# One turn of attention outputs for two or three heads instead of one for each, and the first head's shift rows ahead of the second head's masks

## Chip, core and metric

One Trainium2 chip, and of it one core. The metric is the device time of one execution in microseconds (us), given as the median of the runs. Five engines work side by side and wait for each other by semaphores: TensorE (PE), VectorE (DVE), ScalarE (ACT), GpSimd (POOL) and SyncE (SP), which here only issues DMAs.

## What is computed

`x` is 16 batches of 512 rows of 128 features. A feed-forward step with quantized operands, attention with 16 heads of 8 features, and the feed-forward step again:

```python
scores = jnp.einsum('bhqd,bhkd->bhqk', Q, K) / scale        # hd = 8, L = 512
mask = _tpms_mask(L, phase, threshold, temperature)         # one 512x512 mask per head, the same for all batches
scores = scores + TPMS_WEIGHT * jnp.log(mask + 1e-06)[None]
attn = jax.nn.softmax(scores, axis=-1)
out = jnp.einsum('bhqk,bhkd->bhqd', attn, V)
out = out.transpose(0, 2, 1, 3).reshape(B, L, H)
return out @ Wo + bo
...
x = x + 0.5 * _L0_ffn_ref(_layernorm(x, axis=-1), L0_ffn_weight, L0_ffn_bias)
x = x + _L0_attn_ref(_layernorm(x, axis=-1), ...)
x = x + 0.5 * _L0_ffn_ref(_layernorm(x, axis=-1), L0_ffn_weight, L0_ffn_bias)
```

## The kernel before

A prologue computes the logarithms of the 16 masks (ACT, `ln_mask`, L825) and stores each to DRAM (`store_mask`, SP), since its place in the big buffer `BIG` is used for other things later: the places of heads 9 to 12 become the second half of `E`, the exponentials of every odd turn, one batch each. The same prologue projects the first four batches and stores their split queries and keys (`q_parts`, `k_parts`).

Then follow 64 **head turns** `m` = 0 to 63: four quarters of four batches (`j` = 0 to 3), 16 heads each. A turn has eight steps `k`, two for each batch, one for each half ("pair") of the 512 keys:

- DVE copies the log mask into the four banks of `S_PS` (`seed`, L1227): two copies for pair 0 once exponential 6 of the turn before is done, two for pair 1 once exponential 7 is.
- PE adds the scores on top (`scores`, L1656), two matmuls a step. ACT takes the exponential of 1,024 elements a partition into `E` (`exp_step`, L777). Only when exponential `k` has read its banks can the scores of step `k+2` be added.
- At the odd steps PE also multiplies the exponentials of the turn before with the values (`weighted`, L1670): four matmuls, one for each batch, into strips of the bank `O_PS` that start at partitions 0, 32, 64 and 96. Float32 matmuls appear as two records each, so such a set is eight records. A strip has nine rows: eight features and the sum of the exponentials, which comes from a column of ones in the values `VX`.
- Two turns later the output of the head is **turned**: ACT copies `O_PS` to `OTS` (`o_copy`, L786) ahead of exponential 0, PE transposes it in four pieces into `R_PS` (`turn_o`, L1679) at step 1 ahead of the scores, and DVE takes reciprocals of the sums and multiplies (`o_norm`, L1240 and L1242) into `AT`. Only after the copy may PE write the next head's output to `O_PS`.

The order of all work on each engine is written out: at fixed ticks (eight to a turn) each engine's program has its pieces of the neighbouring quarters' layer norms, quantization, projections and output products (`background`, the tables `FIRST`, `LATE`, `SECOND`, `LAST`). Engines work strictly in that order.

The attention starts when PE has the stack of queries and keys of head 0 in `KT` and `QT`. POOL issues these six loads (`load_stack(pool, 0)`), and behind them, when DVE has signalled `bound_copied`, four small loads of head 0's **shift rows** from `OTS` (L659). SP meanwhile stores the masks of heads 9, 10, 11 and 12, and then loads head 1's stack. ACT may write the first exponential of turn 1 when all four of these masks are stored:

```python
if k == 0 and m < 2:
    lnm_stored(act, (6, 9)[m])
```

## Time and profile before

| | |
|---|---|
| median of 3 runs | 875.57 us (873.08 to 876.89) |
| the profiled execution | 872.85 us, of which the span from first to last instruction is 871.0 us |
| PE busy | 741.7 us (85% of the span) |
| ACT busy | 669.0 us (77%) |
| DVE busy | 569.6 us (65%) |
| POOL busy | 192.8 us (22%) |
| first exponential of turn 0 begins | 132.64 us |
| exponentials (L777) | 512, of 1,024 ns |
| mean granted TensorE clock | 0.952 of 2.4 GHz |

Busy times are the union of an engine's records; a matmul record holds its way through the array, so that neighbouring records overlap and a busy PE is not a full one. "[0.31 <-PE S_PS L1656]" behind a row says that the engine stood idle for 0.31 us before it, and that the instruction of that line ended the wait. PEld is PE's weight load, SPq a DMA issue on SP.

### The profile page before, as it was taken

The page shows a single profiled execution, that of the slowest core. Times are in us where ns is not written, and L with a number is a line of the kernel's source. Part 1 is how long each engine was busy: PE and PEld are TensorE (multiplying, and loading weights), DVE is VectorE, ACT ScalarE, POOL GpSimd, SP SyncE. Part 2 cuts the span into 40 slices and gives each one's busy share as a digit, 9 for nine tenths or more (in the row PEclk, how much of TensorE's full clock was granted, in tenths as well). Part 3 has the DMA queues.
Part 4 walks back from the last instruction along what each step waited for, and adds up shares of the span by engine and source line. Part 5 has one row for each costly group of instructions (what it writes and reads, how often), then busy time and mean ns, then how long its engine had stood idle before and what let it go on. Part 6 is the DMA issues. An engine that isn't in the chain of part 4 may idle for free.

```text
span 871.0 us, 13076 instructions
## 1 busy us (share of the span) xinstructions
PE 741.7 (85%) x4355; PEld 260.3 (30%) x4355; DVE 569.6 (65%) x1464; ACT 669.0 (77%) x799; POOL 192.8 (22%) x167
## 2 busy tenths in 40 slices
PE   0575808999998999999999999999999998999844
PEld 0142401333233323333332233223322332331234
DVE  8968885757989746899783565985423458433265
ACT  1567667788887888888888888887888887888711
POOL 0404762003443203164140031441200002000011
PEclk9986856999999999999999999999999999999987
DMA  5539588854666574756857547668676555456101
GB/s 148 124 124 340 199 295 283 284 178 156 201 203 219 184 201 166 194 177 177 249 186 235 175 138 217 195 184 236 199 234 181 172 176 183 145 189 205 38 2 53
DMA packets 56166, 162.11 MB, mean 186 GB/s; under 512 B 14210, under 2 KB 24594, under 8 KB 45674
## 3 DMA queue, kind: packets, MB, share of 16 engines
q1 hardware_dynamic: 51740, 154.36, 57.8%
q0 software_dynamic: 1904, 5.94, 2.0%
q10 hardware_dynamic: 2446, 0.89, 0.5%
q8 instruction: 37, 0.61, 0.3%
q14 instruction: 39, 0.32, 0.1%
HBM read 117.86 MB, written 43.29 MB: 185 GB/s over the span
## 4 chain that ended last, share of the span: by engine, by line
PE 54%; DVE 22%; ACT 11%; issue 9%; DMA 2%; POOL 1%; SPq 0%; DVEq 0%; POOLq 0%; ACTq 0%
PE S_PS L1656 20%; PE O_PS L1670 18%; ACT BIG L777 9%; PE F_PS L1557 5%; DVE S_PS L1227 5%; PE R_PS L1679 3%; PE F_PS L1552 2%; DVE SC L1064 1%; PE P_PS L1557 1%; PE P_PS L1594 1%; DVE ST L954 1%; DVE XC L1109 1%; DVE BIG L1054 1%; PE P_PS L1598 1%; DMA BIG<-OTS 1%
## 5 line engine op out<-in xcount | busy, mean ns | idle before, releaser
L777 ACT ACTIVATE BIG<-S_PS 128x1024 f32<-128x1024 f32 x512 | 508.7, 1024 | 107.0 <-PE S_PS L1656 104.9
L1656 PE MATMUL S_PS<-BIG 98*128 98x512 bf16 x1024 | 311.1, 389 | 40.1 <-DMA BIG<-OTS 15.4
L1227 DVE COPY S_PS<-BIG 128x512 f32<-128x512 f32 x256 | 159.6, 687 | 178.1 <-ACT BIG L777 175.9
L1670 PE MATMUL O_PS<-BIG,VX 128*9 128x512 f32 x2048 | 269.2, 599 | 1.2 <-ACT OTS L786 1.2
L1656 PEld LDWEIGHTS S_PS<-BIG 98*128 98x128 bf16 x1024 | 79.3, 98 | 294.0 <-ACT BIG L777 138.0
L601 POOL TENSOR_TENSOR XDT<-PART 128x512 bf16<-128x512 f32 x24 | 28.9, 1202 | 293.5 <-ACT PART L742 293.5
L1670 PEld LDWEIGHTS O_PS<-BIG,VX 128*9 128x9 f32 x2048 | 30.8, 88 | 103.3 <-issue 99.1
L578 POOL TENSOR_TENSOR X<-X,BFH 128x512 f32<-128x512 f32 x16 | 24.1, 1528 | 149.8 <-DVE BIG L1054 120.3
L818 ACT ACTIVATE BIG<-S_PS,TEMP 128x1024 f32<-128x1024 f32 x32 | 34.1, 1112 | 21.1 <-PE S_PS L1843 20.7
L578 POOL TENSOR_TENSOR BIG<-BIG,BFH 128x512 f32<-128x512 f32 x16 | 19.9, 1270 | 129.1 <-DVE BIG L1054 111.8
L786 ACT ACTIVATE OTS<-O_PS,CON 128x512 f32<-128x512 f32 x64 | 44.1, 689 | 4.4 <-PE R_PS L1679 4.4
L617 POOL TENSOR_TENSOR PART<-PART 128x512 bf16<-128x512 f32 x28 | 36.6, 1306 | 37.6 <-DVE PART L1135 37.6
L1679 PE MATMUL R_PS<-IDENT,OTS 128*128 128x128 f32 x256 | 40.3, 281 | 1.8 <-ACT OTS L786 1.8
L1843 PE MATMUL S_PS<-PART 36*128 36x512 bf16 (+1 forms) x32 | 14.1, 556 | 29.9 <-DMA PART<-trig_parts 27.8
L610 POOL TENSOR_TENSOR PART<-PART 128x512 f32<-128x512 f32 x28 | 35.1, 1254 | 10.6 <-DVE PART L1129 8.3
L711 ACT ACTIVATE XDT<-F_PS 128x512 f32<-128x512 f32 x38 | 22.6, 594 | 18.5 <-PE F_PS L1552 18.5
L1679 PEld LDWEIGHTS R_PS<-IDENT,OTS 128*128 128x128 f32 x256 | 27.7, 141 | 18.4 <-issue 15.2
L1557 PE MATMUL F_PS<-WDT,XDT 128*128 128x128 f32 x208 | 31.9, 300 | 0.0
L1557 PEld LDWEIGHTS F_PS<-WDT,XDT 128*128 128x128 f32 x208 | 27.9, 206 | 12.7 <-ACT XDT L711 7.3
L825 ACT ACTIVATE BIG<-BIG,CON 128x2048 f32<-128x2048 f32 x16 | 30.7, 1987 | 0.0
L1552 PE MATMUL F_PS<-IDENT,BIG 128*128 128x128 f32 x112 | 17.9, 284 | 14.0 <-DVE BIG L1090 10.2
L1240 DVE RECIPROCAL RD<-R_PS 128x16 f32<-128x16 f32 x64 | 16.3, 255 | 17.6 <-PE R_PS L1679 17.1
(197 smaller groups left out, 771.1 us busy)
## 6 DMA issues: line engine op xcount, KB each, us to landing
BIG<-ln_masks SPq DMA_DIRECT2D x62, 1024.0 KB, 6.5
ln_masks<-BIG SPq DMA_DIRECT2D x16, 1024.0 KB, 5.5
BIG<-q_parts SPq DMA_DIRECT2D x63, 192.0 KB
BIG<-k_parts SPq DMA_DIRECT2D x63, 144.0 KB
BIG<-q_parts SPq DMA_DIRECT2D x63, 128.0 KB
q_parts<-PART SPq DMA_DIRECT2D x9, 768.0 KB, 3.8
k_parts<-PART SPq DMA_DIRECT2D x18, 384.0 KB, 4.5
BIG<-k_parts SPq DMA_DIRECT2D x63, 96.0 KB
```

Source lines behind the costliest of these rows:

```text
L578: pool.tensor_tensor(Y, Y, bias[:, None, :].to_broadcast((128, T, H)), ALU.add).then_inc(s[name], 1)
L610: pool.tensor_tensor(F_, F_, hi, ALU.subtract).then_inc(s[f"{q}_r1"], 1)
L617: pool.tensor_tensor(P_[2], F_, P_[1], ALU.subtract).then_inc(s[f"{q}_lo"], 1)
L777: act.activation(E[:, m % 2, j, 2 * pair:2 * pair + 2, :], S_PS[:, pair, :, :], ACT.Exp, scale=LOG_WEIGHT)\
L786: act.activation(OTS[:, :], O_PS[:, :], ACT.Identity, bias=CON[:, 2:3]).then_inc(s["o_copied"], 1)
L818: act.activation(stage(h)[:, 1024 * pair:1024 * pair + 1024].rearrange("p (k l) -> p k l", l=L), S_PS[:, t % 2, :, :], ACT.Sigmoid, scale= ...
L1227: ve.tensor_copy(S_PS[:, pair, i, :], LNM[:, slot, 2 * pair + i, :]).then_inc(s["seeded"], 1)
L1552: mm = pe.transpose(dst[:, 128 * t:128 * t + 128], src[:, t, :], IDENT[:, :])
L1557: mm = pe.matmul(dst[:, 128 * t:128 * t + 128], lhsT[:, 128 * t:128 * t + 128], rhs[:, :], start=True, stop=True)
L1656: mm = pe.matmul(S_PS[:, pair, i, :], KT[0:ALL_ROWS, slot, K_COL[j], 128 * kb:128 * kb + 128], QT[0:ALL_ROWS, slot, j, :], start=False, st ...
L1670: mm = pe.matmul(O_PS[32 * j:32 * j + HD + 1, :], VX[:, slot_of(n), j, kb, h, :], E[:, m % 2, j, kb, :], start=kb == 0, stop=kb == T - 1)
L1679: mm = pe.transpose(R_PS[:, 128 * t:128 * t + 128], OTS[:, 128 * t:128 * t + 128], IDENT[:, :])
```

## The change

**Bunches.** The 16 turns of a quarter fall into six bunches of 3, 3, 3, 3, 2 and 2 turns, and each bunch is turned once, two turns after its last head: 24 turns instead of 64. The heads of a bunch lie below each other in a strip of `O_PS`. For this the stationary operand of the first head of a bunch of three takes 27 columns of the values, its own nine and the 18 ahead of them in memory; it fills rows 0 to 26 of a strip, of which rows 18 to 26 are wanted. The second takes 18 columns and writes over rows 0 to 17, the third takes nine. `VX` gets a pad of 18 columns ahead (`VXP`), and the rows of `Wo` are put in the order in which the heads now stand in `AT`. `o_norm` handles two or three heads at once. A head that is not its bunch's first need not wait for a copy of `O_PS`.

**Start.** The four loads of head 0's shift rows go from POOL's queue to SP's, behind the store of mask 9 and ahead of head 1's stack; masks 10, 11 and 12 are stored behind that. The exponentials of turn 1 wait for the masks batch by batch. In the prologue's list for PE, two mask tiles are computed ahead of `project_k(0, 1)` instead of behind it, and one that stood ahead of `norms_q(0, 1)` stands ahead of `turn_xn(0, 2)`.

```diff
-FIRST_LOADS = 16 * (2 * len(GROUPS) + T)
+FIRST_LOADS = 16 * 2 * len(GROUPS)
...
+BUNCHES = ((0, 2), (3, 5), (6, 8), (9, 11), (12, 13), (14, 15))
+NB = len(BUNCHES)
+MOST = max(b - a + 1 for a, b in BUNCHES)
+VPAD = (MOST - 1) * (HD + 1)
+LAST_HEADS = [b for a, b in BUNCHES]
...
+        def bunch_of(m):
+            return m // NH * NB + len([b for b in LAST_HEADS if b < m % NH])
...
+        def turned_in(m):
+            return bunch_of(m - 2) if m >= 2 and (m - 2) % NH in LAST_HEADS else None
...
-            for h in range(9, 13):
-                store_mask(h)
-
+            store_mask(9)
+
+            sp.wait_ge(s["bound_copied"], 1)
+            for t in range(T):
+                sp.dma_start(QT[QK_ROWS:ALL_ROWS, 0, :, 128 * t:128 * t + 128],
+                             CB4[T * head_of(0) + t:T * head_of(0) + t + 1, :, :, :]).then_inc(s["first_shift"], 16)
             load_stack(sp, 1)
+            store_mask(10)
             load_shift(sp, 1)
-            sp.wait_ge(s["first_stack"], FIRST_LOADS)
+            store_mask(11)
+            store_mask(12)
             store_mask(8)
...
             load_stack(pool, 0)
-
             pool.wait_ge(s["bound_copied"], 1)
-            for t in range(T):
-                pool.dma_start(QT[QK_ROWS:ALL_ROWS, 0, :, 128 * t:128 * t + 128],
-                               CB4[T * head_of(0) + t:T * head_of(0) + t + 1, :, :, :]).then_inc(s["first_stack"], 16)
...
-                if k == 0 and m < 2:
-                    lnm_stored(act, (6, 9)[m])
+                if k == 0 and m == 0:
+                    lnm_stored(act, 6)
+                if pair == 0 and m == 1:
+                    lnm_stored(act, 9 + j)
...
-                    if k == 0 and m >= 2:
-                        o_copy(m - 2)
+                    if k == 0 and turned_in(m) is not None:
+                        o_copy(turned_in(m))
...
-                turned = R_PS[:, :].rearrange("p (t g r) -> p t g r", t=T, g=QB)
-                ve.reciprocal(RD[:, :, :], turned[:, :, :, HD]).then_inc(s["o_rd"], 1)
-                ve.wait_ge(s["o_rd"], m + 1)
-                TT(AT[:, slot_of(n), :, :, HD * h:HD * h + HD].rearrange("p j t d -> p t j d"),
-                   turned[:, :, :, 0:HD], RD[:, :, :, None].to_broadcast((128, T, QB, HD)), ALU.mult)\
+                turned = R_PS[:, :].rearrange("p (t g r) -> p t g r", t=T, g=QB)[:, :, :, 0:size * (HD + 1)]\
+                    .rearrange("p t g (s d) -> p t g s d", s=size)
+                ve.reciprocal(RD[:, :, :, 0:size], turned[:, :, :, :, HD]).then_inc(s["o_rd"], 1)
+                ve.wait_ge(s["o_rd"], u + 1)
+                TT(AT[:, slot_of(n), :, :, HD * first:HD * last + HD].rearrange("p j t (s d) -> p t j s d", s=size),
+                   turned[:, :, :, :, 0:HD], RD[:, :, :, 0:size, None].to_broadcast((128, T, QB, size, HD)), ALU.mult)\
...
-                    if past(m):
-                        pe.wait_ge(s["o_copied"], m)
+                    if past(u) and m % NH == first:
+                        pe.wait_ge(s["o_copied"], u)
                 pe.wait_ge(s["e_ready"], STEPS * m + STEPS - 1 + kb // 2)
                 for j in range(QB):
-                    mm = pe.matmul(O_PS[32 * j:32 * j + HD + 1, :], VX[:, slot_of(n), j, kb, h, :],
+                    at = VPAD + ((j * T + kb) * NH + head_of(m)) * (HD + 1)
+                    mm = pe.matmul(O_PS[32 * j:32 * j + ahead + HD + 1, :],
+                                   VXP[:, slot_of(n), at - ahead:at + HD + 1],
                                    E[:, m % 2, j, kb, :], start=kb == 0, stop=kb == T - 1)
...
-            turn_o(last - 1)
-            turn_o(last)
+            turn_o(bunch_of(last))
```

On SP, at the end of the prologue, before the change (`ln_masks<-BIG` is a mask's store, the six `k_parts` and `q_parts` are head 1's stack, `shift_rows` its shift rows):

```order
L435 DMA ln_masks<-BIG 128x2048 x5
L390 DMA BIG<-k_parts 48x1536
L393 DMA BIG<-q_parts 48x2048
L390 DMA BIG<-k_parts 32x1x1536
L393 DMA BIG<-q_parts 32x1x2048
L390 DMA BIG<-k_parts 16x1x1536
L393 DMA BIG<-q_parts 16x1x2048
L403 DMA BIG<-shift_rows 2x4x512
L435 DMA ln_masks<-BIG 128x2048
L450 DMA BIG<-ln_masks 128x2048
```

The same place on SP after the change (`BIG<-OTS` are head 0's shift rows):

```order
L458 DMA ln_masks<-BIG 128x2048 x2
L570 DMA BIG<-OTS 2x4x128 x4
L413 DMA BIG<-k_parts 48x1536
L416 DMA BIG<-q_parts 48x2048
L413 DMA BIG<-k_parts 32x1x1536
L416 DMA BIG<-q_parts 32x1x2048
L413 DMA BIG<-k_parts 16x1x1536
L416 DMA BIG<-q_parts 16x1x2048
L458 DMA ln_masks<-BIG 128x2048
L426 DMA BIG<-shift_rows 2x4x512
L458 DMA ln_masks<-BIG 128x2048 x3
L473 DMA BIG<-ln_masks 128x2048
```

Three mask stores moved from ahead of head 1's stack to behind it, and the four small loads stand ahead of it.

On PE, turns 1 and 2 before the change (`O_PS` is `weighted`, `R_PS<-IDENT,OTS` is `turn_o`, the others are scores and background):

```order
L1670 MATMUL O_PS<-BIG,VX 9x512 x4
L1656 MATMUL S_PS<-BIG 128x512 x2
L1679 MATMUL R_PS<-IDENT,OTS 128x128 x4
L1656 MATMUL S_PS<-BIG 128x512 x2
L1670 MATMUL O_PS<-BIG,VX 9x512 x4
L1656 MATMUL S_PS<-BIG 128x512 x4
```

The same place on PE after the change:

```order
L1705 MATMUL O_PS<-BIG,VXP 27x512 x4
L1687 MATMUL S_PS<-BIG 128x512 x4
L1705 MATMUL O_PS<-BIG,VXP 18x512 x4
L1687 MATMUL S_PS<-BIG 128x512 x4
L1705 MATMUL O_PS<-BIG,VXP 18x512 x4
```

The four transposes between the scores of steps 0 and 1 are gone in this turn, and the strips have 27 and 18 rows.

On PE, the end of the attention before the change:

```order
L1656 MATMUL S_PS<-BIG 128x512 x4
L1670 MATMUL O_PS<-BIG,VX 9x512 x20
L1679 MATMUL R_PS<-IDENT,OTS 128x128 x8
L1552 MATMUL F_PS<-IDENT,BIG 128x128 x4
L1552 MATMUL P_PS<-IDENT,BIG 128x128 x4
```

The same place after the change:

```order
L1687 MATMUL S_PS<-BIG 128x512 x4
L1705 MATMUL O_PS<-BIG,VXP 18x512 x4
L1705 MATMUL O_PS<-BIG,VXP 9x512 x16
L1715 MATMUL R_PS<-IDENT,OTS 128x128 x4
L1581 MATMUL F_PS<-IDENT,BIG 128x128 x4
L1581 MATMUL P_PS<-IDENT,BIG 128x128 x4
```

One turn of four transposes is left of two.

## Rows read from the trace of the kernel before

**Rows 1.** The page, busy time of each engine and its share of the span.

```profile
PE 741.7 (85%) x4355; PEld 260.3 (30%) x4355; DVE 569.6 (65%) x1464; ACT 669.0 (77%) x799; POOL 192.8 (22%) x167
```

**Rows 2.** Timeline, start and length in us, exponential 0 of turn 61, boundary into 62.

```profile
796.79 1.02 ACT L777 ACTIVATE BIG<-S_PS 128x1024 f32<-128x1024 f32 x1 [0.31 <-PE S_PS L1656]
...
804.70 2.47 DVE L1227 COPY S_PS<-BIG 128x512 f32<-128x512 f32 x4 [6.72 <-ACT BIG L777]
...
805.47 0.69 ACT L786 ACTIVATE OTS<-O_PS,CON 128x512 f32<-128x512 f32 x1
...
806.41 0.63 PE L1679 MATMUL R_PS<-IDENT,OTS 128*128 128x128 f32 x4
806.47 1.02 ACT L777 ACTIVATE BIG<-S_PS 128x1024 f32<-128x1024 f32 x1 [0.31 <-PE S_PS L1656]
...
807.22 0.10 PEld L1656 LDWEIGHTS S_PS<-BIG 98*128 98x128 bf16 x1 [0.36 <-DVE S_PS L1227]
...
807.55 1.05 PE L1670 MATMUL O_PS<-BIG,VX 128*9 128x512 f32 x8
```

**Rows 3.** Timeline, the boundary into turn 52.

```profile
702.13 2.64 DVE L1227 COPY S_PS<-BIG 128x512 f32<-128x512 f32 x4 [4.50 <-ACT BIG L777]
...
704.74 0.60 PE L1656 MATMUL S_PS<-BIG 98*128 98x512 bf16 x2
...
705.27 1.05 PE L1670 MATMUL O_PS<-BIG,VX 128*9 128x512 f32 x8
```

**Rows 4.** Timeline, DVE in turn 40, in turn 54, and turn 55's start.

```profile
583.27 0.68 DVE L1159 TENSOR_REDUCE KTOP<-R_PS 16x1 f32<-16x512 f32 x1 [1.10 <-PE R_PS L1617]
...
727.17 0.29 DVE L1242 TENSOR_TENSOR BIG<-R_PS,RD 128x128 f32<-128x128 f32 x1
...
736.41 1.02 ACT L777 ACTIVATE BIG<-S_PS 128x1024 f32<-128x1024 f32 x1 [3.09 <-PE S_PS L1656]
```

**Rows 5.** Timeline, the end of the prologue and the first scores and exponentials.

```profile
114.47 9.56 ACT L825 ACTIVATE BIG<-BIG,CON 128x2048 f32<-128x2048 f32 x5
...
116.35 1.43 DVE L1212 TENSOR_SCALAR OTS<-R_PS 64x128 bf16<-64x128 f32 x7
...
120.84 2.22 POOL L659 DMA_DIRECT2D BIG<-OTS  x4
...
131.57 1.89 PE L1656 MATMUL S_PS<-BIG 98*128 98x512 bf16 x4 [15.40 <-DMA BIG<-OTS]
...
132.64 1.94 ACT L777 ACTIVATE BIG<-S_PS 128x1024 f32<-128x1024 f32 x2 [8.62 <-PE S_PS L1656]
```

**Rows 6.** DMA issues, 55 to 143 us: KB each, us to landing.

```profile
q_parts<-PART POOLq DMA_DIRECT2D x2, 768.0 KB, 4.6
...
q_parts<-BIG POOLq DMA_DIRECT2D x1, 384.0 KB, 2.9
...
BIG<-OTS POOLq DMA_DIRECT2D x4, 2.0 KB, 8.9
```

**Rows 7.** Windows: engines' busy us, TensorE clock, DMA share, GB/s.

```profile
124.00:126.00 2.00, 0.00 (x0) 0.00 (x0) 2.00 (x1) 0.02 (x1) 2.00 (x2) 0.50 1.02 412
```

**Rows 8.** Groups by line and shape: count, busy us, mean ns, idle before.

```profile
L786 ACT ACTIVATE OTS<-O_PS,CON 128x512 f32<-128x512 f32 x64 | 44.1, 689 | 4.4 <-PE R_PS L1679 4.4
...
L1240 DVE RECIPROCAL RD<-R_PS 128x16 f32<-128x16 f32 x64 | 16.3, 255 | 17.6 <-PE R_PS L1679 17.1
...
L1670 PEld LDWEIGHTS O_PS<-BIG,VX 128*9 128x9 f32 x2048 | 30.8, 88 | 103.3 <-issue 99.1 <-ACT BIG L777 4.2
...
L1679 PEld LDWEIGHTS R_PS<-IDENT,OTS 128*128 128x128 f32 x256 | 27.7, 141 | 18.4 <-issue 15.2 <-ACT OTS L786 1.1
...
L1072 DVE RECIPROCAL SC<-SC 128x64 f32<-128x64 f32 x5 | 2.8, 553 | 0.2
```

**Rows 9.** Timeline, the end of the attention.

```profile
825.61 3.62 PE L1670 MATMUL O_PS<-BIG,VX 128*9 128x512 f32 x32 [1.25 <-ACT OTS L786]
...
829.92 0.69 ACT L786 ACTIVATE OTS<-O_PS,CON 128x512 f32<-128x512 f32 x1 [4.40 <-PE R_PS L1679]
```

More of the change, by code:

```diff
@@ L68 @@
 HEAD_ORDER = [0, 8, 1, 2, 3, 4, 5, 6, 7, 9, 10, 11, 12, 13, 14, 15]
+BUNCHES = ((0, 2), (3, 5), (6, 8), (9, 11), (12, 13), (14, 15))
[3 more added lines that the diff above has]
+LAST_HEADS = [b for a, b in BUNCHES]
+ROW_BLOCK = {HEAD_ORDER[i]: a + b - i for a, b in BUNCHES for i in range(a, b + 1)}
 HALF_TILES = 16
@@ L294, in parts_stored, with bunches_before @@
                 engine.wait_ge(s["parts_out_k"], K_STORES * n)
+        def bunch_of(m):
+            return m // NH * NB + len([b for b in LAST_HEADS if b < m % NH])
+        def turned_in(m):
+            return bunch_of(m - 2) if m >= 2 and (m - 2) % NH in LAST_HEADS else None
+        def bunches_before(m):
+            return len([i for i in range(max(m, 0)) if i % NH in LAST_HEADS])
         def stack_name(m):
@@ L1227, in seed, with o_norm @@
                     ve.tensor_copy(S_PS[:, pair, i, :], LNM[:, slot, 2 * pair + i, :]).then_inc(s["seeded"], 1)
-            def o_norm(m):
-                n, h = m // NH, head_of(m)
-                ve.wait_ge(s["o_turned"], m + 1)
-                if m % NH == 0:
+            def o_norm(u):
+                n, (first, last) = u // NB, BUNCHES[u % NB]
+                size = last - first + 1
+                ve.wait_ge(s["o_turned"], u + 1)
+                if u % NB == 0:
                     if not is_short(n):
@@ L1261, in attention @@
                     m = q * NH + tick // STEPS
-                    if k == 1 and m >= 2:
-                        o_norm(m - 2)
+                    if k == 1 and turned_in(m) is not None:
+                        o_norm(turned_in(m))
                     background(q, tick)
@@ L1660, in weighted @@
             def weighted(m, kb):
-                n, h = m // NH, head_of(m)
+                n, u = m // NH, bunch_of(m)
+                first, last = BUNCHES[u % NB]
+                ahead = (HD + 1) * (last - m % NH)
                 if kb == 0:
@@ L1769, in attention @@
                         background(q, tick)
-                    if k == 1 and m >= 2:
+                    if k == 1 and turned_in(m) is not None:
                         c = CHAINS[q]
```

66 lines of the change are left out of this document (37 added, 29 removed).

## The prediction

> **What bounds the kernel now.** I read the page first. PE is busy 85% of the span, ACT 77%, DVE 65% [rows 1]. None of the three is full, so the reader should ask at each turn of the attention which engine is late, and not which one works most. For that I went through the timeline turn by turn.
>
> Take the boundary into turn 62, one of eight turns late in the quarters that have no background work. DVE begins its four mask copies at 804.70, right behind exponential 6, and needs 2.47 us. ACT does the output copy of 0.69 us from 805.47 to 806.16 and then stands for 0.31 us: exponential 0 begins at 806.47, when PE has added the scores to the second copied bank. PE's four transposes lie at 806.41 to 807.04. The last scores of step 1 are released at 807.22 by the fourth mask copy (804.70 + 2.47 = 807.17), and `weighted` begins at 807.55 [rows 2]. So the chain through the boundary is exponential 6, four mask copies, scores, `weighted`. ACT's output copy and PE's transposes both lie inside it, and neither is what ends last. After the chain come the pauses of ACT that follow from `weighted` standing between scores on PE; they are not touched.
>
> The start of the attention is bound by something else. ACT has its last mask logarithm at 114.47 + 9.56 = 124.03, yet PE's first scores wait until 131.57 for the last of four small loads that POOL issues at 120.84 to 123.06, and ACT waits until 132.64, 8.62 us idle [rows 5]. These loads of 2 KB take 8.9 us to land [rows 6], while the DMA engines are full (share 1.02 at 412 GB/s) [rows 7] with the stores of masks 10 to 12, head 1's stack and head 0's.
>
> **The change, part by part.** Forty turns of 64 vanish: 40 x 689 ns = 27.6 us of ACT, 160 transposes on PE, and on DVE 40 x (255 + 290 ns) = 21.8 us [rows 8, 4]. What is left is wider. Reciprocals of 16 elements take 255 ns and of 64 take 553 ns, so 6.2 ns an element: 48 take about 0.45 us, 32 about 0.35 us [rows 8]. For the product of 384 elements instead of 128 in 0.29 us [rows 4] I bound the growth by nothing and by three times, and take 0.56 us. A turn of three heads so costs DVE 0.46 us more, 16 times, one of two heads 0.23 us more, 8 times: 9 us of the 21.8 come back.
>
> *The output copies: nothing.* At every turn's start ACT waits for PE even with the copy in its place, as in [rows 2]. Without it the wait grows from 0.31 to 1.00 us and ends at the same time. If mask copies and scores came 1.0 us earlier, that cover would be gone and each copy would be worth up to 0.69 us.
>
> *The transposes: 1.9 us.* In most turns the second score of step 1 comes 0.06 us after the fourth mask copy and `weighted` 0.38 us after it, as in [rows 2], whatever PE did before. There the transposes are free. In 13 turns that lose theirs PE is late, because an output product or a projection stands ahead: at turn 52 (the pattern) the copies end at 702.13 + 2.64 = 704.77 and `weighted` begins at 705.27, 0.50 after them instead of 0.38 [rows 3]. I take 0.15 us each (0.12 to 0.22). The upper bound is the whole of 40 x 0.6 us, the lower nothing.
>
> *DVE's normalization: 3.0 us.* It pays only where DVE itself is late for the next mask copies. At turn 55 ACT waits 3.09 us for them, and DVE worked without a pause from its normalization (0.26 + 0.29 us) on; there 0.55 us comes back [rows 4]. Nine turns that lose a normalization in the turn before have such a lateness (10, 13, 22, 25, 28, 38, 39, 41, 55). In four DVE runs through: 3 x 0.55 + 0.33. In the other five it also waits for PE's norms, as 1.10 us in turn 40 [rows 4], which can swallow all; I take 0.2 us each. Against this the wider ones that stay could delay the copies of turns 8 and 14, by 0.46 us each at most; DVE waits for PE in both turns before, so I take nothing. Bounds: 0 to 5.
>
> *The wider weights: -1.0 us.* The matmul streams 512 columns as before. Only its weight load grows, and of a set of eight the first load shows, between the last score and the first product. On average over a quarter a strip gets 126 / 16 = 7.9 more columns. The rows: 9 columns 88 ns, 128 columns 141 ns, both float32 [rows 8], so 0.45 ns a column; three of four sets a turn are on the path, 192 x 3.5 ns = 0.7 us, rounded up to 1.0. A proportional price is the upper bound: 9.8 ns a column gives 77 ns x 192 = 14.8 us. I stay with the low end, since the row with fourteen times the columns is only 1.6 times as long. The Trainium skill ("TensorE: Matmul & The Clock Gate", LDWEIGHTS) puts the load at the number of columns over 1.2 per ns, whatever the rows; by that alone 7.9 columns are 6.6 ns, 1.3 us in all, and the trace's 88 ns for nine columns shows that most of a load isn't in that rule.
>
> *The start: 7.6 us.* SP has stored mask 9 when DVE has the bounds copied (116.35 + 1.43 = 117.8 [rows 5]), and issues the four small loads at some 0.6 us each, to 120.2. Nothing is ahead of them now but head 0's stack, whose last load POOL issues just before 120.84 [rows 5]. In the same stretch 384 KB of POOL's land in 2.9 us where little else moves and 768 KB in 4.6 us [rows 6]. So the stack is there at 123.7 to 125.4, and the first exponential follows the scores by 1.07 us at half clock [rows 5]. I take 125.0, against 132.64. Bounds: ACT free at 124.03 gives 8.6 us; loads that take 8.9 us as before give 130.8, 1.8 us. Behind the four loads SP's order moves head 1's stack and masks 10 to 12, needed from about 134 on (125.0, eight exponentials of 1.02 us, 1.0 us of wait), then every 2.1 us; 3 MB at 412 GB/s are 7.6 us, from about 125. So they are just in time. What is late next is ACT's own logarithms.
>
> The Trainium skill ("DMA: Bandwidth & Descriptors", Issuing engines are not separate DMA queues) speaks against a gain from the queue as such: all issuers share 16 DMA engines. By that rule the move from POOL to SP gives only issue time, and what counts is the 3 MB of masks no longer ahead; the share of 1.02 agrees. Were those stores not moved, the sum would have 1.8 us in this place.
>
> *The end: 1.6 us.* Turn 63's products now don't wait for the copy of turn 62's, 1.25 us, and one of two turns is gone: ACT's last copy begins right behind the products, at about 825.61 - 1.25 + 3.62 + 0.07 = 828.05 instead of 829.92 [rows 9]. The last normalization is 0.23 us longer: 1.87 - 0.23.
>
> **The sum.** 7.6 + 1.9 + 3.0 + 1.6 - 1.0 = 13.1 us from 872.85 of the profiled execution, of which 871.0 is span: 859.8. The median of the runs shown is 2.7 us above that execution, so I forecast 862.5. A measurement of this kernel can tell about 0.5%, 4.4 us, from no change.
>
> **Rivals.**
> - *The start stays* (0.13). The small loads still take 8 to 9 us, because head 1's stack (six loads, 672 KB) now runs beside them, or turn 1's exponentials wait for masks 11 and 12, whose stores stand behind a load that needs `first_out_shift`. For it: the DMA engines' share of 1.02 [rows 7]. Against: 3 MB less. Then 1.8 to 4 us remain of 7.6: 866 to 868.5.
> - *The freed time counts in full* (0.12). If PE and ACT follow each other more closely than I read, the transposes give 0.4 us in each of 40 turns and DVE 5 us: 14 us more than the middle terms, 848. Against it: the 0.31 us of ACT's wait and the 0.36 us of PE's for DVE [rows 2], the same in all turns without background.
> - *Almost nothing* (0.08). The middle gives 0, the weights cost 3 to 6 us, and the start only half: 869 to 876. For it: most of DVE's late turns wait for PE too.
> - *Slower* (0.04). The four strips of a set run side by side today: 32 records of 0.6 us in 3.62 us [rows 9]. If strips of 18 and 27 rows in a bank hinder each other, each such set grows; 160 sets are wide, 120 of them on the path. It decides from 14.1 / 120 = 0.12 us a set. One after another they would take four times as long, 2.7 us more a set, and the kernel about 1,180 us. Against it: strips lie 32 partitions apart and 27 rows fit.
>
> **Chances and range.** My forecast as worked out, 856 to 866, has 0.63. Faster by over 0.5% (below 871.2) takes it, the start that stays, and the full gain: 0.88. Within 0.5%: 0.08. Slower: 0.04. The range reaches down halfway to the full gain and up over the start that stays: 854 to 869.
>
> **What would show it.** Right: the first exponential at 124 to 126; ACT's wait ahead of exponential 0 about 1.0 us in turns without a copy and the period of quiet turns still 9.68 us (796.79 to 806.47 [rows 2]); 24 turns on L1715; mask copies of turns 13, 22 and 55 some 0.5 us less late; weight loads of 27 columns near 95 ns. Wrong: quiet turns that fall to 9.2 us or less, records of `weighted` over 0.6 us, or exponentials of turn 1 released by a mask's store.

## The result, and the profile after

| | before | after |
|---|---|---|
| median of 7 runs each, side by side | 875.62 us | 868.58 us (864.6 to 871.24) |
| the profiled execution; its span | 872.85; 871.0 us | 868.58; 866.7 us |
| first exponential of turn 0 | 132.64 us | 127.37 us |
| exponential 0 of turn 3 | 166.47 us | 167.56 us |
| exponential 0 of turn 63 | 816.15 us | 812.62 us |
| from there to the span's end | 54.85 us | 54.08 us |

The ratio is 0.991, 95% interval 0.9886 to 0.9934: 7.0 us faster, where 13.1 us were forecast. The two profiled executions stand 4.3 us apart, and the table divides these: the start of the attention is 1.1 us *later*, turns 3 to 63 are 4.6 us shorter (649.68 to 645.06), the end is 0.8 us shorter.

The page's busy times answer to [rows 1]: ACT has 23.7 us less to do, PE 11.1, DVE 8.9.

```profile
PE 730.6 (84%) x4195; PEld 247.8 (29%) x4195; DVE 560.7 (65%) x1385; ACT 645.3 (74%) x759; POOL 190.4 (22%) x163
```

The timeline of the start, ACT and PE, answers to [rows 5]. The scores' matmuls begin 5.25 us earlier than before, since the small loads have landed. The last two rows hold the new thing: turn 2, which began at 154.36 before, begins at 155.97, and ACT has been idle for 8.31 us.

```profile
117.06 9.56 ACT L851 ACTIVATE BIG<-BIG,CON 128x2048 f32<-128x2048 f32 x5
...
126.32 1.86 PE L1687 MATMUL S_PS<-BIG 98*128 98x512 bf16 x4 [7.56 <-DMA BIG<-OTS]
...
127.37 1.94 ACT L803 ACTIVATE BIG<-S_PS 128x1024 f32<-128x1024 f32 x2 [0.75 <-PE S_PS L1687]
...
154.90 1.89 PE L1687 MATMUL S_PS<-BIG 98*128 98x512 bf16 x4 [7.55 <-DMA BIG<-shift_rows]
...
155.97 1.94 ACT L803 ACTIVATE BIG<-S_PS 128x1024 f32<-128x1024 f32 x2 [8.31 <-PE S_PS L1687]
```

PE names who it waits for: the last load of head 2's stack, issued by SP at 142.37. The windows say why that load needs 12.5 us (busy us with the number of instructions of PE, PEld, DVE, ACT and POOL, then TensorE's granted clock, the DMA engines' share, GB/s). From 130 on the 16 DMA engines are full: by the DMA issues from 127 to 143 us, six mask stores and a mask load of 1 MB each go out beside a stack of 672 KB. In the last window PE does nothing.

```profile
130.00:135.00 5.00, 4.30 (x9) 0.53 (x8) 2.15 (x18) 4.58 (x6) 0.00 (x0) 0.50 1.01 423
135.00:140.00 5.00, 4.23 (x13) 0.73 (x14) 4.89 (x15) 2.80 (x3) 0.00 (x0) 0.50 1.01 362
140.00:145.00 5.00, 5.00 (x24) 0.95 (x22) 3.64 (x4) 3.49 (x6) 3.79 (x4) 0.74 0.98 346
145.00:150.00 5.00, 2.28 (x16) 0.37 (x12) 4.91 (x7) 2.64 (x3) 1.18 (x1) 0.95 1.03 367
150.00:155.00 5.00, 0.10 (x1) 0.10 (x2) 4.85 (x8) 0.00 (x0) 0.00 (x0) 0.50 1.03 235
```

A quiet turn reads as forecast. In the timeline of turns 61 to 63 the period is 9.69 and 9.68 us as in [rows 2]. Turn 61 and 63 still have a copy and ACT waits 0.32 and 0.31 us; turn 62 has none and ACT waits 0.89.

```profile
793.25 1.02 ACT L803 ACTIVATE BIG<-S_PS 128x1024 f32<-128x1024 f32 x1 [0.32 <-PE S_PS L1687]
...
802.94 1.02 ACT L803 ACTIVATE BIG<-S_PS 128x1024 f32<-128x1024 f32 x1 [0.89 <-PE S_PS L1687]
...
812.62 1.02 ACT L803 ACTIVATE BIG<-S_PS 128x1024 f32<-128x1024 f32 x1 [0.31 <-PE S_PS L1687]
```

The groups by line and shape answer to [rows 8]: what a wide set costs DVE, and what a wide weight load costs.

```profile
L1271 DVE TENSOR_TENSOR BIG<-R_PS,RD 128x384 f32<-128x384 f32 x16 | 8.9, 557 | 0.6
L1269 DVE RECIPROCAL RD<-R_PS 128x48 f32<-128x48 f32 x16 | 7.3, 456 | 0.7 <-PE R_PS L1715 0.5
...
L1705 PEld LDWEIGHTS O_PS<-BIG,VXP 128*27 128x27 f32 x512 | 9.7, 105 | 25.8 <-issue 23.2 <-ACT BIG L803 2.5
L1705 PEld LDWEIGHTS O_PS<-BIG,VXP 128*18 128x18 f32 x768 | 12.9, 96 | 36.9 <-issue 36.1 <-ACT BIG L803 0.8
L1705 PEld LDWEIGHTS O_PS<-BIG,VXP 128*9 128x9 f32 x768 | 11.8, 88 | 37.1 <-issue 36.7 <-ACT BIG L803 0.4
```

The end answers to [rows 9]: from turn 63's exponential 0 to the start of the last copy 11.75 us, 13.77 before.

```profile
819.81 4.49 PE L1705 MATMUL O_PS<-BIG,VXP 128*18 128x512 f32 x40
...
824.37 0.69 ACT L812 ACTIVATE OTS<-O_PS,CON 128x512 f32<-128x512 f32 x1 [2.94 <-PE O_PS L1705]
```

### The profile page after: what moved, and what is told of

Read it like the earlier page. It is cut to its first block, busy times and chain, and to the rows that moved or that the text cites. A ratio compares the mean times of both kernels' runs of the same rounds, so it can differ in the third digit from the quotient of the medians.

```text
span 866.7 us, 12515 instructions
## 1 busy us (share of the span) xinstructions
PE 730.6 (84%) x4195; PEld 247.8 (29%) x4195; DVE 560.7 (65%) x1385; ACT 645.3 (74%) x759; POOL 190.4 (22%) x163
## 4 chain that ended last, share of the span: by engine, by line
PE 48%; DVE 23%; ACT 14%; issue 10%; DMA 2%; SPq 1%; POOL 1%; DVEq 0%; ACTq 0%; POOLq 0%
PE S_PS L1687 18%; PE O_PS L1705 17%; ACT BIG L803 10%; DVE S_PS L1254 7%; PE F_PS L1586 4%; PE F_PS L1581 2%; DMA BIG<-shift_rows 1%; ACT BIG L851 1%; PE R_PS L1715 1%; PE P_PS L1623 1%; DVE ST L981 1%; DVE SC L1091 1%; DVE BIG L1081 1%; PE P_PS L1581 1%; PE P_PS L1586 1%
## 5 line engine op out<-in xcount | busy, mean ns | idle before, releaser
L1705 PE MATMUL O_PS<-BIG,VXP 128*18 128x512 f32 (+2 forms) x2048 | 271.8, 604 | 0.0
L1705 PEld LDWEIGHTS O_PS<-BIG,VXP 128*18 128x18 f32 (+2 forms) x2048 | 34.3, 95 | 99.8 <-issue 96.0
L1156 DVE CAST PART<-PART 128x512 bf16<-128x512 f32 x28 | 22.8, 813 | 5.1 <-ACT PART L766 4.4
L988 DVE TENSOR_SCALAR VE<-MV 128x4 f32<-128x4 f32 x48 | 22.7, 473 | 1.6
L729 ACT ACTIVATE RS<-VE 128x8 f32<-128x8 f32 (+1 forms) x19 | 4.0, 209 | 25.5 <-DVE VE L988 18.2
L981 DVE BATCH_NORM_STATS2 ST<-X 128x6 f32<-128x128 f32 x96 | 20.9, 280 | 0.6
```

What stands on the lines that cost most here:

```text
L981: c(ve.bn_stats(ST[:, k, QB * j + t, :], xj[:, t, :]), wait=False)
L1705: mm = pe.matmul(O_PS[32 * j:32 * j + ahead + HD + 1, :], VXP[:, slot_of(n), at - ahead:at + HD + 1], E[:, m % 2, j, kb, :], start=kb == 0 ...
```

## The experiments

My theory after the traces: the bunches carry the whole gain, because DVE and the transposes pay where they were late; the new start earns 5.3 us and loses them at turn 2, since head 2's stack is late. Rivals are in each expectation. All ratios are to the kernel before, run beside.

### The two halves apart

The changed kernel with the old start (the waits of turn 1's exponentials, the four small loads and the tiles' order as before; the core of the edit):

```diff
-            store_mask(9)
-            sp.wait_ge(s["bound_copied"], 1)
-            for t in range(T):
-                sp.dma_start(QT[QK_ROWS:ALL_ROWS, 0, :, 128 * t:128 * t + 128], ...
-            load_stack(sp, 1)
-            store_mask(10)
-            load_shift(sp, 1)
-            store_mask(11)
-            store_mask(12)
+            for h in range(9, 13):
+                store_mask(h)
+            load_stack(sp, 1)
+            load_shift(sp, 1)
+            sp.wait_ge(s["first_stack"], FIRST_LOADS)
```

> The changed kernel with its start as it was before: the shift rows loaded by POOL, masks 9 to 12 stored first, the old order of projection tiles. What stays of the change are the bunches of three heads. Theory: in the changed kernel's trace turn 3 begins 1.1 us later than before and all from there to the end is 5.4 us shorter (649.68 to 645.06 from turn 3 to turn 63, and 0.8 behind), so the bunches carry the whole gain: first exponential at 132 to 134, turn 2 at 154 to 156, 5 to 6 us below the kernel before, 867.5 to 870.5. Rival, that the start carries some 5 of the 7 us between the medians: only 2 us below the kernel before, about 873.5.

Measured: 867.54 us, ratio 0.9905 (0.988 to 0.993). The first exponential is at 131.96, turn 2 at 153.70, turn 3 at 164.39, 3.2 us ahead of the changed kernel.

The kernel before with the new start put in: the same lines the other way, and turn 1's exponentials waiting batch by batch.

> The kernel before with the new start alone: shift rows on SP ahead of masks 10, 11, 12 and 8, exponentials of turn 1 waiting batch by batch; no bunches, old order of projection tiles. Theory, that the 5.3 us by which the first exponential comes earlier are given back where turn 2 waits for head 2's stack behind mask stores in SP's queue: first exponential at 126 to 127, turn 2 at 154 to 156 with a wait of 7 to 9 us ahead of it, time within 1.5 us of the kernel before (874 to 877). Rival, that the start's gain is real and something in the bunches hides it: turn 2 at about 148, 5 to 7 us below the kernel before, 869 to 870.5.

Measured: 875.46 us, ratio 0.9996 (0.9978 to 1.0014). Two rows of ACT's timeline repeat the changed kernel's picture, with no bunches in it:

```profile
126.84 1.94 ACT L780 ACTIVATE BIG<-S_PS 128x1024 f32<-128x1024 f32 x2 [0.36 <-PE S_PS L1661]
...
155.84 1.02 ACT L780 ACTIVATE BIG<-S_PS 128x1024 f32<-128x1024 f32 x1 [8.31 <-PE S_PS L1661]
```

So the new start as written is worth nothing, and the bunches carry the whole of what the medians show.

### Why the stack is late: order in the queue, or bytes

First, masks 13 and 14 are stored one head later:

```diff
                 if more and m >= 1:
                     load_mask(m + 1)
-                    if m == 1:
-                        for h in range(13, 15):
-                            store_mask(h)
                     load_stack(sp, m + 1)
...
                 if m == 2:
-                    store_mask(15)
+                    for h in range(13, 16):
+                        store_mask(h)
```

> The changed kernel, but masks 13 and 14 are stored behind head 3's stack and not ahead of head 2's. Theory: head 2's stack is issued at 133.5 to 142.4 with only masks 11, 12, 8 and the load of mask 2 ahead of it in the queue, lands at 145 to 147, and turn 2 begins at 148 to 149 in place of 155.97: 6 to 8 us below the changed kernel, 861 to 863. Rival A, that the issue times of SP and not the bytes ahead set the landing (the last load is issued at 142.4 because the stack waits for the scores of turn 0): turn 2 at 154 to 156, about 868. Rival B, that the wait goes on to turn 3, whose mask load is issued at 143 and landed at 158.09: turn 2 at 148, turn 3 at 164 or later, 864 to 867.

Measured: 866.88 us, ratio 0.9897 (0.9869 to 0.9926). Turn 2 begins at 149.73, with 3.94 us of wait left, turn 3 at 161.49 with no more than its usual 1.34. But two megabytes moved are two megabytes elsewhere: turn 4 waits for its stack instead.

```profile
149.73 1.94 ACT L801 ACTIVATE BIG<-S_PS 128x1024 f32<-128x1024 f32 x2 [3.94 <-PE S_PS L1685]
...
175.19 1.02 ACT L801 ACTIVATE BIG<-S_PS 128x1024 f32<-128x1024 f32 x1 [2.83 <-PE S_PS L1685]
```

The theory had the place right. Its numbers (turn 2 at 148, 861 to 863 us) did not come; rival B had the time (864 to 867) and the carried wait right and its turn wrong.

Second, the order in SP's queue is taken out of it. POOL issues head 2's stack, in its own queue with nothing ahead:

```diff
             pool.memset(VX[:, 1, :, :, :, HD:HD + 1], 1.0).then_inc(s["vx_ones"], 1)
+            load_stack(pool, 2)
+            load_shift(pool, 2)
```

> The changed kernel, but head 2's stack and shift rows are issued by POOL, behind its memset at 128.6 and ahead of its next additions at 141.2; the bytes and their order in time stay, masks 13 and 14 are still stored at 133.6 and 134.8 by SP. Theory, that the order within SP's own queue makes the stack late: POOL's loads land 3 to 4 us after their issue, at 144 to 146, turn 2 begins at about 148, 861 to 863. Rival, that the 16 DMA engines serve what is outstanding whichever queue it came from, so that 5 MB of masks delay it all the same: the last load lands at 152 to 155, turn 2 at 154 to 156, 867 to 869.

Measured: 868.05 us, ratio 0.9902 (0.9881 to 0.9924). Turn 2 begins at 150.41 after 4.59 us of wait. The theory had POOL's loads land 3 to 4 us after their issue. The DMA issues from 126 to 143 us (KB each, us to landing) say otherwise: POOL's 8 KB, behind nothing but the stack in POOL's own queue, take 13.0 us.

```profile
BIG<-q_parts POOLq DMA_DIRECT2D x1, 64.0 KB, 12.3
BIG<-k_parts POOLq DMA_DIRECT2D x1, 48.0 KB, 12.1
...
BIG<-shift_rows POOLq DMA_DIRECT2D x1, 8.0 KB, 13.0
```

In the changed kernel the same load took 12.5 us. What the move does give is the time of issue: POOL issues the load at 136.30, SP did at 142.37 (1.9 of these 6.1 us stem from a first exponential that is earlier here), and turn 2 begins 5.6 us earlier than in the changed kernel. Neither the theory (148) nor the rival (154 to 156) had that turn; the rival had the time. Without the 1.9 us these are 3.6, of which 0.8 are left at turn 6, since the bytes are the same: ACT waits 2.32 us at turn 4 and 2.41 at turn 5, 0.82 and 0.61 in the changed kernel. So its place in SP's queue makes head 2's stack late by its issue time, and what the 16 DMA engines still have to move makes the rest of it, and of the turns behind. The Trainium skill ("DMA: Bandwidth & Descriptors", Issuing engines are not separate DMA queues) says that all issuers share these engines and a second one saves only issue time, and these rows agree. The prediction cited that rule for head 0's loads and never asked it of head 2's.

So bytes had to leave the stretch. Mask 8 goes behind head 2's stack, 13 and 14 behind head 3's, 15 behind head 4's, and two inputs of 1 MB that are needed much later are loaded in turns 4 and 8:

```diff
-                    if m == 1:
-                        for h in range(13, 15):
-                            store_mask(h)
...
+                if m == 1:
+                    store_mask(8)
                 if m == 2:
+                    store_mask(13)
+                    store_mask(14)
+                if m == 3:
                     store_mask(15)
+                if m == 4:
+                    lnm_stored(sp, 15)
+                    load_x(2)
+                if m == 8:
                     sp.wait_ge(s["val_ready"], 2 * HALF_TILES)
                     load_x(3)
-                if m == 3:
-                    lnm_stored(sp, 15)
-                    load_x(2)
...
             store_mask(12)
-            store_mask(8)
```

> The changed kernel with 4 MB moved behind later stacks: mask 8 is stored behind head 2's stack, masks 13 and 14 behind head 3's, mask 15 behind head 4's, and the input of batches 2 and 3 loaded in turns 4 and 8 in place of 3 and 2. Theory, that from 130 to 170 the 16 DMA engines themselves are full (share 1.0 in the windows of the runs so far) and every stack is late by the bytes ahead of it: turn 2 begins at 147 to 148 with a wait of about 1.5 us, turn 4 no longer waits for its stack, turn 6 at 191 to 193 (200.5 in the changed kernel, 196.4 with two stores moved), time 860 to 863. Rival, that the bytes come back as waits of turns 3 to 9 (masks 4 to 7 late, or batch 2's input late for its statistics at turn 6): turn 10 no earlier than with two stores moved, 865 to 868.

Measured: 859.41 us (857.71 to 861.15), ratio 0.9813 (0.9793 to 0.9834). It beats both kernels, the changed one by 9 us of the medians. Its timeline of ACT: the first exponential follows the last logarithm at once, turn 2 begins at 147.57, turn 3 at 158.26 (9.3 us earlier than in the changed kernel), and turn 6 at 191.16. In the windows from 140 to 150 the DMA engines have air where they were full.

```profile
125.84 1.91 ACT L805 ACTIVATE BIG<-S_PS 128x1024 f32<-128x1024 f32 x2
...
147.57 1.02 ACT L805 ACTIVATE BIG<-S_PS 128x1024 f32<-128x1024 f32 x1 [1.70 <-PE S_PS L1689]
...
158.26 1.03 ACT L805 ACTIVATE BIG<-S_PS 128x1024 f32<-128x1024 f32 x1 [1.39 <-PE S_PS L1689]
...
140.00:145.00 5.00, 4.93 (x33) 0.97 (x32) 4.03 (x4) 4.66 (x8) 4.64 (x4) 0.94 0.78 271
145.00:150.00 5.00, 3.38 (x22) 0.73 (x15) 4.82 (x12) 2.91 (x3) 0.00 (x0) 1.00 0.42 136
```

Is that the moved bytes alone? The same moves with the old start:

> The kernel with the bunches only (old start), and the same 4 MB moved behind later stacks as in the run that took 859.4 us. Theory, that the moved bytes are worth something only to the new start, since turn 2 of the old start waited just 1.4 us: first exponential at 132 to 133, turn 2 at 154, time 866 to 868, as the bunches alone (867.5); the new start is then worth 7 to 8 us once its stack is not late. Rival, that the moved bytes themselves give the gain: 860 to 863.

Measured: 870.15 us, ratio 0.9932 (0.9908 to 0.9956), no better than the bunches alone. So the moves without the new start give nothing, the new start without the moves gives nothing (868.58), and both together give 8.1 us against the bunches alone (867.54 - 859.41). The traces of these two runs place 6.1 us of it: the first exponential at 131.96 and 125.84, turn 3 at 164.39 and 158.26. The 10.7 us between 870.15 and 859.41 overstate it. This run's first exponential is late, at 136.24, with POOL's four loads issued from 122.29 on among full DMA engines; in the run with the bunches only, whose program is the same up to there, it is at 131.96. Why these 4.3 us came is open.

The projection tiles' new order was the remaining suspect for the 2.6 us by which ACT's logarithms end later (126.62 against 124.03):

```diff
-                     (2, project_k, 1), (1, turn_xn, 2), (1, project_v, 1), (0, project_q, 2), (1, norms_k, 1),
-                     (1, norms_q, 1),
+                     (0, project_k, 1), (2, turn_xn, 2), (1, project_v, 1), (0, project_q, 2), (1, norms_k, 1),
+                     (2, norms_q, 1),
```

> The same as the run with 4 MB moved, but with the order of the projections' tiles as before the change (third tile's turn ahead of the second tile's keys). Theory, that the new order costs about 0.5 us of what ACT's mask logarithms lose ahead of 117 us: the last logarithm ends 0.3 to 0.7 us earlier, and the time is 0.5 us lower, within what a median tells (860 to 863). Rival, that the whole 2.3 to 2.6 us by which the changed kernel's logarithms ended later come from the tile order: last logarithm at 124, time 2 us lower.

Measured: 859.79 us, ratio 0.9823 (0.9803 to 0.9844), with the first exponential at 127.42, not earlier. The order can't be told apart from nothing, and the new start with the old order (the second run) ends its logarithms at 126.47. Over the nine traces with the new start and the new order the first exponential lies anywhere from 125.20 to 127.43. The logarithms end at 123.17 to 124.65 in the three traces with the old start and at 124.00 to 126.96 in the eleven with the new one, so the 2.6 us are either spread or something in the new start; no run separates these.

### The middle: which engine's work was worth something

From turn 17 on most periods repeat from run to run within 0.05 us where nothing is changed, so single turns can be read. Each number is the difference of two starts of exponential 0 in a run's timeline, in us; the last column is turn 16 to turn 63.

Turn 55 is an exception, and the last column holds it too. TensorE is granted the lower of its two levels (1.2 of 2.4 GHz) in a part of it, and how large a part differs: with the changed kernel's bunches it takes 10.27 us at a mean granted clock of 1.00 (in the run with the bytes moved and the old start) and 11.75 at 0.85, and before the change 11.10 at 0.89. Turn 13 is another: 12.58 us at 0.86 in the run with the bunches only, 10.97 at 1.00 in the changed kernel. Nothing is read from these two. A late load can also fall into a single turn: in the run with the bytes moved and the old start PE waits for shift rows in turns 25 and 38, 0.39 and 0.49 us, and they take 12.77 and 11.83 us.

```
turn                      14     25     30     38     41     54     55     62   16 to 63
before                 10.24  12.75  10.02  11.89  12.74  12.46  11.10   9.68   503.30
after                   9.74  12.21   9.89  11.40  12.26  11.02  11.70   9.68   499.81
copies put back         9.74  12.21   9.89  11.40  12.25  11.02  11.59   9.68   499.62
DVE's work put back     9.74  12.70   9.89  11.89  12.32  13.76  11.31   9.68   504.19
transposes doubled     10.24  12.22   9.89  11.40  12.26  11.03  11.98   9.68   505.41
bunches of two         10.24  12.96   9.89  11.41  12.99  11.02  11.52   9.68   501.26
27 columns for all      9.79  12.23   9.93  11.40  12.29  11.02  11.54   9.71   500.06
```

Copies put back on ACT:

```diff
                     if k == 0 and turned_in(m) is not None:
                         o_copy(turned_in(m))
+                    elif k == 0 and m >= 5:
+                        act.wait_ge(s["o_turned"], bunches_before(m - 1))
+                        act.activation(OTS[:, :].rearrange("p (t n) -> p t n", t=T),
+                                       IDENT[:, None, :].to_broadcast((128, T, 128)), ACT.Identity, bias=CON[:, 2:3])
```

> The changed kernel, and in the 37 turns from turn 5 on that have lost their output copy ACT copies 128x512 elements again, from the identity in SBUF to OTS, ahead of the turn's first exponential; its result is not used. Theory, that an output copy stood in ACT's wait for the scores and cost nothing: ACT's wait ahead of those exponentials shrinks from 0.89 to about 0.3 us, turns 16 to 61 take 480.4 us as without it (within 0.5), time as the changed kernel's, 867 to 870. Rival, that ACT's freed time counted: 37 copies at 0.4 to 0.67 us, 15 to 25 us more, 883 or above.

Measured: 867.30 us, ratio 0.9911 (0.9886 to 0.9937); 37 copies of 0.72 us, 26.6 us of ACT, whose results are not used, cost nothing in any turn. In turn 62 the copy stands in the wait, which falls back from 0.89 to 0.28 us:

```profile
800.38 0.72 ACT L860 ACTIVATE OTS<-IDENT,CON 128x512 f32<-128x512 f32 x1
801.38 1.02 ACT L803 ACTIVATE BIG<-S_PS 128x1024 f32<-128x1024 f32 x1 [0.28 <-PE S_PS L1691]
```

DVE's work put back, with results that are not used (they go to `OTS`, so that the output copies that are left wait for them):

```diff
                     if k == 1 and turned_in(m) is not None:
                         o_norm(turned_in(m))
+                    elif k == 1 and m >= 5:
+                        parts = OTS[:, 0:144].rearrange("p (t g r) -> p t g r", t=T, g=QB)
+                        ve.reciprocal(OTS[:, 144:160]..., IDENT[:, 0:16]...).then_inc(s["junk"], 1)
+                        ve.wait_ge(s["junk"], 2 * put_back(m + 1) - 1)
+                        TT(parts[:, :, :, 0:HD], IDENT[:, 0:128]..., IDENT[:, 0:16]...to_broadcast((128, T, QB, HD)), ALU.mult).then_inc(s["junk"], 1)
```

> The changed kernel, and in the same 37 turns DVE does a reciprocal of 128x16 and a product of 128x128 elements again, as long as the removed normalization's, from SBUF into OTS, behind one another and ahead of the turn's other work; the results are not used. Theory of the prediction, that DVE's normalization gave 3.0 of the 3.9 us in the middle because it delayed seeds in the turns full of work: turns 16 to 61 take 482.5 to 483.3 us in place of 480.4 (483.9 before), quiet turns still 9.68, time 870 to 871.5. Rival A, that the transposes on TensorE gave it: 480.4 to 481.0, time as the changed kernel's. Rival B, that DVE's time counts in full (0.6 us each): 20 us more.

Measured: 875.43 us, ratio 0.999 (0.997 to 1.0009), 6.9 us more than the changed kernel; turns 16 to 61 take 484.82 us. That is more than the change took away, so the rise must be taken apart. In turns 25 and 38 the removed 0.5 us come back within 0.05: there DVE's work is the whole gain. In turn 54, 2.74 us come back where 1.44 had gone, because my copy of the work was not a true one. Its product takes both operands from SBUF and 1.20 us beside POOL's addition; before, with one operand in PSUM, it took 0.29 us beside the same addition [rows 4]. DVE's and POOL's timeline of turn 54 in this run:

```profile
729.63 5.04 POOL L609 TENSOR_TENSOR BIG<-BIG,BFH 128x512 f32<-128x512 f32 x4 [104.42 <-DVE BIG L1087]
...
729.88 1.20 DVE L1304 TENSOR_TENSOR OTS<-IDENT 128x128 f32<-128x128 f32 x1
731.00 1.23 DVE L1060 TENSOR_TENSOR RS<-RS 128x16 f32<-128x16 f32 x1
```

Some 2 us more come from the crowded start: PE waits 2.94 us for turn 5's shift rows, a DMA. So the run bounds DVE's share from above and gives it cleanly only in single turns: 0.5 us each in turns 9, 25 and 38, and turns 14, 30 and 41 don't need DVE to be shorter.

Where DVE's work is taken away ahead of an operation that runs beside one of POOL, its length alone says little. Turn 21 lost a normalization of 0.5 us, and its mask copies begin 9.35 us after its start, 9.36 before. The timelines of DVE and POOL, first before, then after the change:

```profile
370.90 1.16 POOL L617 TENSOR_TENSOR PART<-PART 128x512 bf16<-128x512 f32 x1
371.29 0.29 DVE L1242 TENSOR_TENSOR BIG<-R_PS,RD 128x128 f32<-128x128 f32 x1
371.50 0.85 DVE L1129 CAST PART<-PART 128x512 bf16<-128x512 f32 x1
```

```profile
370.80 1.16 POOL L645 TENSOR_TENSOR PART<-PART 128x512 bf16<-128x512 f32 x1
370.90 1.34 DVE L1156 CAST PART<-PART 128x512 bf16<-128x512 f32 x1
```

Counted from the turn's start, DVE's next operation begins 0.5 us earlier, takes 0.5 us longer, and ends where it did, 0.3 us behind POOL's operation. Turn 12 has the same picture (0.79 us and 1.26).

Transposes doubled in the 24 turns that still have them:

```diff
-                for t in range(T):
+                for t in [*range(T), *range(T)]:
                     mm = pe.transpose(R_PS[:, 128 * t:128 * t + 128], OTS[:, 128 * t:128 * t + 128], IDENT[:, :])
```

> The changed kernel with the four transposes of each of the 24 bunches done twice. Theory of the prediction, that a set of transposes costs 0.13 to 0.15 us in a turn behind an output product and nothing in a quiet one: quiet turns at 9.68, each turn with a set that also has a turn of a tile about 0.15 longer, 0.5 to 1.5 us from turn 16 to turn 63. Rival A, that DVE hides them everywhere: less than 0.2 us. Rival B, that a set costs its own duration everywhere (about 0.4 us): 7 us and more over the 19 sets.

Measured: 876.68 us, ratio 1.001 (0.999 to 1.003), 8.1 us more, and 5.6 us from turn 16 to turn 63: far above the theory (0.5 to 1.5), below rival B's 7. Turn 61, quiet, takes 9.98 us instead of 9.69. The timelines of PE in that turn, first of the changed kernel, then of the doubled one, show the cover and its end. With one set, 0.63 us, the scores follow at 793.65, in two parts that still await the mask copies (0.74 us). With two sets they begin 0.90 us after the first transpose instead of 0.46 and run through, and `weighted` begins 1.42 us after it instead of 1.14.

```profile
793.19 0.63 PE L1715 MATMUL R_PS<-IDENT,OTS 128*128 128x128 f32 x4
793.65 0.74 PE L1687 MATMUL S_PS<-BIG 98*128 98x512 bf16 x2
794.33 1.05 PE L1705 MATMUL O_PS<-BIG,VXP 128*18 128x512 f32 x8
```

```profile
801.09 1.06 PE L1715 MATMUL R_PS<-IDENT,OTS 128*128 128x128 f32 x8
801.99 0.60 PE L1687 MATMUL S_PS<-BIG 98*128 98x512 bf16 x2
802.51 1.05 PE L1705 MATMUL O_PS<-BIG,VXP 128*18 128x512 f32 x8
```

A quiet turn so hides one set whole and not a second. Removing the first is worth 0 there, adding another costs 0.29. The doubling does not measure what the removal gave.

Bunches of two heads (`BUNCHES = tuple((i, i + 1) for i in range(0, NH, 2))`):

> The changed kernel with eight bunches of two heads a batch in place of six: 32 sets of copy, transposes and normalization in place of 24, and weights of 9 and 18 columns alone. Theory, that what is gained goes by the sets removed that stood in the path (32 removed in place of 40) and the columns cost at most 0.07 us a turn: turns 16 to 63 take 500.0 to 501.0 us (499.8 with bunches of three, 503.3 before), turn 54 or 55 changes most, time 868.5 to 870.5. Rival, that the wider weights cost as much as predicted or more: 499.0 to 499.6.

Measured: 872.1 us, ratio 0.9955 (0.9935 to 0.9975), 3.5 us more than with bunches of three; turns 16 to 63 take 1.45 us more. Fewer sets are better and the wider weights don't take it back. The rise is more than in proportion to the eight sets, since turns 25 and 41, where a set of two heads falls, become longer than before the change.

Every head's weights 27 columns wide; this kernel leaves out keeping the sums of a bunch's heads apart, which write over one another's rows:

```diff
-                ahead = (HD + 1) * (last - m % NH)
+                ahead = (HD + 1) * (MOST - 1)
```

> The changed kernel with 27 columns of weights for every head, 9 more than the mean of the bunches of three; the sums of a bunch's heads then fall on one another's rows, so that the outputs are not the reference's. Theory, that a column costs what its load takes (0.9 to 1.1 ns, 16 loads a turn, 0.15 us a turn of TensorE's time), and this shows only in the turns where TensorE is late: quiet turns at 9.68, turns 16 to 63 longer by 0.3 to 1.0 us. Rival, that it counts in full in every turn: 9 us more over the kernel, 7 us from turn 16 to turn 63.

Measured: 867.38 us, ratio 0.9901 (0.9871 to 0.9931); turns 16 to 63 0.25 us longer. Quiet turns take 9.71 us in place of 9.68, so a wide load does reach the path, with 0.03 us a turn; turns 17 to 62 without turn 55 take 0.65 us more. 2,048 loads of 104 ns cost nothing that a median can tell.

## Why the prediction was right, and where it was not

The time, 868.58, lies at the upper edge of the range (854 to 869), and the kernel is faster as forecast; the gain is half of the 13.1 us. The forecast as worked out, 856 to 866, missed. That the time lies inside is luck: the range reached up over the rival *the start stays*, whose mechanism did not occur. By its terms:

- *The output copies, nothing.* Right, and shown by putting them back. ACT's wait without a copy was forecast at 1.00 us and is 0.89.
- *The transposes 1.9 and DVE's normalization 3.0 us, weights -1.0.* The sum was 3.9 and 4.6 us came between turns 3 and 63, in part by luck, for the turns are others. The prediction named nine turns whose mask copies DVE delays, by the turn that then begins late; the table above counts the turn before it. Turns 9 and 38 are 0.49 us shorter, where I had taken 0.2, turn 24 0.16, turn 54 1.44 for 0.55; turns 12, 21, 27, 37 and 40 are not shorter at all. So the sign that the mask copies of turns 13 and 22 come 0.5 us less late did not come. The step that failed there is that DVE "runs through": its rows have no gap, but an operation beside one of POOL takes longer, and that took the 0.5 us back (turn 21 above). In turn 54 it went the other way: without the normalization DVE's next operation on 16 elements in SBUF starts ahead of POOL's addition and takes 0.17 us, where it took 0.85 beside it, and the mask copies begin 1.22 us earlier. The other 0.22 us belong to the clock: in the run with two stores later the copies begin at the same place as in the changed kernel, the turn's mean granted clock is 0.95 in place of 1.00, and it takes 11.24 us. Against this, turns 14, 25 and 41 are 0.5 us shorter each and were not on the list. For turn 25 that is DVE; 14 and 41 came back neither with the copies nor with DVE's work. The same holds for 0.13 us in turns such as 30. By elimination these would be the transposes', but no run put one set back into those turns. An exact split of the 4.6 us stays open.
- *The wider weights.* Mis-sized: 27 columns take 105 ns, 0.95 ns a column, twice the slope I read from 128 columns; but what reaches the path is little, 0.03 us in a quiet turn for ten columns more in the mean. The price of the Trainium skill ("TensorE: Matmul & The Clock Gate", LDWEIGHTS), columns over 1.2 per ns and so an estimate of 0.83 ns a column, is near this slope, and says nothing of the 88 ns that nine columns take.
- *The end 1.6 us.* To the last copy the gain was 2.0 us (1.87 forecast); 1.2 us of it went in the epilogue, where the windows from the last copy to the end have a mean granted clock of 0.75 against 0.80 before; that the clock took them is likely and not shown. 0.8 us is left.
- *The start 7.6 us.* This step failed. Its first half held: the small loads land, the first exponential is at 127.37 and in other runs at 125.2 to 127.4, for 125.0 forecast. What failed is "What is late next is ACT's own logarithms". "So they are just in time" held for head 1's stack and masks 10 to 12, of which I spoke. I followed the moved bytes up to mask 12 and stopped. Behind it on the same 16 engines stood masks 8, 13 and 14, the load of mask 2, and head 2's stack, which must land before turn 2. That stack's deadline had moved forward with the start, by 5.3 us, and the bytes ahead of it had not shrunk. ACT waited 8.31 us at turn 2 in place of 1.69, and of the term of 7.6 us nothing was left at turn 3. With the bytes moved behind it the first exponential is at 125.84, 6.8 us earlier than before and 6.1 earlier than with the bunches only, and the 6.1 us are still there at turn 3, so that most of the term comes.

The rival *the start stays* gave nearly the time that came, 866 to 868.5, by a mechanism that did not: its small loads were not slow, and turn 1's exponentials waited for no mask. The rival *the freed time counts in full* is excluded by quiet turns that stay at 9.68 us, *almost nothing* by the middle's 4.6 us, and *slower* by sets of 18 columns, and of 27 in the last run above, that take 1.05 to 1.06 us in a quiet turn, as sets of nine did [rows 2].

## What to carry to other kernels

When a start is brought forward, list every transfer with a deadline in the next several turns and add up the bytes ahead of each; where the DMA engines are full, the gain moves to the first one that is late, and issuing one of them earlier or on another queue only moves the wait to the next (turns 4 and 5 here); moving bytes out of the stretch creates room. Judge a removed operation turn by turn: one that lies in a wait is worth nothing however long it is (26.6 us of copies here), and one ahead of late work on its own engine is worth its whole length only if nothing between them waits in turn. A row without a gap does not prove that: compare the length of the same operation elsewhere. Before a single turn is compared, compare its granted clock. Don't take the price of removing work from a run that doubles it: a turn that hides one set need not hide two.

## What the runs showed of the hardware

- A DVE product of 128x128 elements with both operands in SBUF took 0.29 us alone and 1.20 us beside POOL's addition of 128x512 elements, and an operation of 16 elements 1.23 us there in place of 0.17; with one operand in PSUM the product took 0.29 us beside the same addition. The Trainium skill ("SBUF — State Buffer", SBUF: two separate sides) has DVE and GpSimd exclude each other on a shared pair of ports when both of DVE's inputs lie in SBUF; these rows agree.
- A cast of 128x512 elements on DVE took 0.43 us alone, 0.85 us when it began 0.6 us into a POOL operation of 128x512 elements, and 1.34 when it began 0.1 us into it; the last two ended 0.3 us behind POOL's.
- A load of 8 KB that POOL issued needed 13.0 us to land, in 17 us in which SP issued eight transfers of 1 MB; on SP's own queue it needed 12.5.
- The same turn of the loop took 10.27 us at a mean granted clock of 1.00 and 11.75 at 0.85.
- Weight loads of 9, 18 and 27 float32 columns took 88, 96 and 105 ns.
